# Residual sum and normalising steps at other places on VectorE, feed-forward products at the end of each pair's work on TensorE

## What is computed

```python
for i in range(DEPTH):        # DEPTH = 6, HEADS = 16, DIM_HEAD = 64, WINDOW = 32
    x = attn_layer(shift_tokens(x), Wqkv[i], q_scale[i], k_scale[i], Wo[i]) + x
    x = ffn_layer(shift_tokens(x), ln_g[i], ln_b[i], W1[i], b1[i], W2[i], b2[i]) + x

def ffn_layer(x, g, bln, W1, b1, W2, b2):
    mu = x.mean(-1, keepdims=True)
    var = ((x - mu) ** 2).mean(-1, keepdims=True)
    xn = (x - mu) / jnp.sqrt(var + 1e-05) * g + bln
    hg = xn @ W1 + b1                      # 128 -> 2 * 341
    a, gate = jnp.split(hg, 2, -1)
    return a * jax.nn.gelu(gate, approximate=False) @ W2 + b2
```

## Time and profile before

| | us |
|---|---|
| median of 3 runs | 6589.64 |
| lowest, highest | 6587.38, 6609.08 |
| the profiled execution | 6594.14 |
| its span | 6592.5 |
| PE busy in the span | 5401.5 |
| DVE busy in the span | 4045.7 |
| ACT busy in the span | 2755.0 |

### The profile page before, as it was taken

The page is one execution under the profiler, slowest core; times in us unless marked ns, Lnnn a source line. Parts: engine busy times, 40 slices in busy tenths (PEclk is TensorE's granted clock), DMA queues, the critical chain, the costliest instruction groups (busy, mean ns, idle before and its releaser), DMA issues. The chain is left out here.

```text
span 6592.5 us, 170288 instructions
## 1 busy us (share of the span) xinstructions
PE 5401.5 (82%) x71376; PEld 3458.5 (52%) x71376; DVE 4045.7 (61%) x6338; ACT 2755.0 (42%) x5035; POOL 2357.1 (36%) x2148
## 2 busy tenths in 40 slices
PE   6877778686868768888888888888888888888884
PEld 4756657484846554444444444444444444444442
DVE  6464656555564656666666666666666666666662
ACT  3132232313132315555555454455555555455552
POOL 2132222222222324444444444444444444444440
PEclk8787878796878879999999999999999999999997
DMA  0000000000000002222222222222222222222221
GB/s 17 4 1 4 1 4 1 4 1 4 3 2 4 1 34 60 57 55 67 62 56 56 60 64 56 53 64 62 57 57 64 64 56 56 59 63 55 55 50 37
DMA packets 255851, 252.33 MB, mean 38 GB/s; under 512 B 29680, under 2 KB 248688, under 8 KB 254704
## 3 DMA queue, kind: packets, MB, share of 16 engines
q1 hardware_dynamic: 255088, 241.29, 14.5%
HBM read 29.90 MB, written 4.19 MB: 5 GB/s over the span
## 5 line engine op out<-in xcount | busy, mean ns | idle before, releaser
L1245 POOL TENSOR_TENSOR turn<-prod 128x512 f32<-128x512 f32 x768 | 977.4, 1273 | 1872.0 <-PE banks L1018 998.7
L988 PE MATMUL banks<-w2s,xs 128*128 128x512 f32 x2304 | 1290.0, 643 | 62.6 <-DVE xs L1317 54.8
L1285 DVE TENSOR_TENSOR prod<-banks,tabs 128x1024 f32<-128x1024 f32 x768 | 936.6, 1219 | 138.7 <-ACT sq L1132 137.3
L1254 POOL TENSOR_TENSOR turn<-turn,rs 128x512 f32<-128x512 f32 x768 | 794.4, 1055 | 450.7 <-ACT rs L1149 449.2
L1132 ACT ACTIVATE sq<-banks 128x512 f32<-128x512 f32 x768 | 458.5, 597 | 967.4 <-PE banks L988 967.0
L583 POOL TENSOR_TENSOR ao<-at,msk 128x512 f32<-128x512 f32 x288 | 390.7, 1367 | 1013.7 <-PE banks L360 534.1
L1018 PEld LDWEIGHTS banks<-msk,turn 128*128 128x128 f32 x3072 | 349.2, 142 | 533.2 <-issue 518.2
L1296 DVE TENSOR_REDUCE ss<-sq 128x8 f32<-128x512 f32 x768 | 519.4, 676 | 1.5
L1066 PE MATMUL banks<-ot,w2s 128*128 128x512 f32 x768 | 413.3, 621 | 126.8 <-DVE y L1354 123.3
L988 PEld LDWEIGHTS banks<-w2s,xs 128*128 128x128 f32 x2304 | 382.4, 201 | 235.4 <-DVE xs L1317 61.9
L1018 PE MATMUL banks<-msk,turn 128*128 128x128 f32 x3072 | 478.6, 279 | 2.5 <-ACT ot L1177 1.6
(11 more groups left out here) (204 smaller groups left out, 9741.6 us busy)
## 6 DMA issues: line engine op xcount, KB each, us to landing
v<-v_tok SPq DMA_DIRECT2D x1152, 132.0 KB, 2.5
v<-v_tok SPq DMA_DIRECT2D x384, 66.0 KB, 2.1
v<-v SPq DMA_DIRECT2D x188, 132.0 KB, 2.5
w2s<-in_weights SPq DMA_DIRECT2D x10, 768.0 KB, 4.8
tabs<-in_rot SPq DMA_DIRECT2D x40, 128.0 KB, 2.6
w2s<-in_weights SPq DMA_DIRECT2D x1, 2713.5 KB, 11.1
w2s<-in_weights SPq DMA_DIRECT2D x10, 256.0 KB, 3.0
xin<-in_x SPq DMA_DIRECT2D x8, 256.0 KB, 3.5
```

The lines of the kernel that those rows point to most:

```text
L988: pe.matmul(a_bank(use), xs[:, t % 2, b * P:(b + 1) * P], w[:, at:at + 512], start=True, stop=True).then_inc(a_done, 1)
L1245: gp.tensor_tensor(turn[:, r % ROTS, :, :].rearrange(halves, s=2), prod[:, r % 2, 0, :, :].rearrange(halves, s=2), prod[:, r % 2, 1, :, :] ...
L1254: gp.tensor_tensor(turn[:, r % ROTS, :, :], turn[:, r % ROTS, :, :], along(rs[:, q % 2, b, :], DH), ALU.mult).then_inc(rot_done, 1)
L1285: v.tensor_tensor(prod[:, r % 2, :, :, :], a_bank(use).rearrange("p (h d) -> p h d", h=HU).unsqueeze(1) .to_broadcast([P, 2, HU, DH]), tab ...
```

## The change

Nothing is added or taken away on any engine but the place of instructions. On PE and in the numbering `a_use` the feed-forward products come after `values`, and with them ACT's part, after its second `take_heads`. On DVE the residual sum is taken out of step 1 and becomes step 0, in pair 0, between the second `sums` and `normalise`; the copies to `xf` stay in pair 1 behind the second `rotate`; the steps 2, 5 and 6 go behind `normalise`; the inverse deviation, scale and shift go from pair 3 to pair 4 (k = 4), between the first `sums` and the second `rotate`.

```diff
@@ a_use, PE's order of the bank's uses
+            if feed:
+                a_use["x", g, 2] = len(a_use)
             for name in ffn_products(g):
                 a_use["c", g // 8 - 1, name] = len(a_use)
-            if feed:
-                a_use["x", g, 2] = len(a_use)
@@ PE
-                        for name in ffn_products(g):
-                            ffn(g // 8 - 1, name)
                         if feed:
                             project(g, 2)
                         if order:
                             turn_heads(order[1])
                         if attend:
                             values(g)
+                        for name in ffn_products(g):
+                            ffn(g // 8 - 1, name)
@@ ACT
-                        if 8 <= g:
-                            ffn(g // 8 - 1, g % 8)
...
                         if order:
                             take_heads(order[1])
+                        if 8 <= g:
+                            ffn(g // 8 - 1, g % 8)
@@ DVE
+                    def carry(t):
+                        if t % NT:
+                            v.tensor_copy(y1[:, :, 0:1], y1[:, :, P:P + 1]).then_inc(carry_done, 1)
+                        else:
+                            v.memset(y1[:, :, 0:1], 0.0).then_inc(carry_done, 1)
+
                     def ffn(t, k):
                         at = t % NT * P + 1
-                        if k == 1:
+                        if k == 0:
+                            carry(t)
                             v.wait_ge(o_done, 8 * t + 8)
-                            if t % NT:
...
                             v.wait_ge(carry_done, t + 1)
                             v.tensor_tensor(y1[:, :, 1:1 + P], blocks(out_bank), y[:, :, at:at + P],
                                             ALU.add).then_inc(res_done, 1)
+                        elif k == 1:
                             v.wait_ge(res_done, t + 1)
...
-                        elif k == 3:
+                        elif k == 4:
                             v.wait_ge(rstd_ready, t + 1)
...
                             sums(g, 0)
+                        if 8 <= g and g % 8 == 4:
+                            ffn(g // 8 - 1, 4)
+                        if feed:
                             rotate(g, 1)
-                        if 8 <= g:
+                        if 8 <= g and g % 8 == 1:
                             ffn(g // 8 - 1, g % 8)
                         if feed:
                             sums(g, 1)
+                        if 8 <= g and g % 8 == 0:
+                            ffn(g // 8 - 1, 0)
                         if attend:
                             normalise(g)
+                        if 8 <= g and g % 8 in (2, 5, 6):
+                            ffn(g // 8 - 1, g % 8)
```

More of the change, by code:

```diff
@@ L1343, in scale_table @@
                         v.tensor_tensor(tile, tile, w[:, W_S:W_1], ALU.mult).then_inc(tab_ready, 1)
+                    def carry(t):
[3 more added lines that the diff above has]
+                            v.memset(y1[:, :, 0:1], 0.0).then_inc(carry_done, 1)
                     def ffn(t, k):
                         at = t % NT * P + 1
-                        if k == 1:
+                        if k == 0:
+                            carry(t)
                             v.wait_ge(o_done, 8 * t + 8)
-                            if t % NT:
-                                v.tensor_copy(y1[:, :, 0:1], y1[:, :, P:P + 1]).then_inc(carry_done, 1)
-                            else:
-                                v.memset(y1[:, :, 0:1], 0.0).then_inc(carry_done, 1)
                             v.wait_ge(carry_done, t + 1)
```

## The result

The changed kernel takes 6361.12 us (median of 4 runs, 6355.04 to 6365.21) beside 6592.37 for the kernel before: ratio 0.9644, 95% interval [0.9624, 0.9664]. That is outside the range of the prediction (6185 to 6345) and 130 us above its number. The profiled execution has a span of 6356.3 us.

A forecast was written before the change was run, and what follows sets the result against it. PE was taken to set the pace, other engines mattering only through its waits. Terms: 123 + 138 + 103 = 364 us saved, 11 given back, 6 gained, so 359 off 6589.6 gives 6231 us; range 6185 to 6345.

The forecast's parts named there:

- the two waits: PE's waits in `output` for the residual sum and before pair 4's scores (L997) go: gains of 123 and 138 us.
- the order of starts by which the residual sum should be hidden: Pair 0: the sum (0.69 us) fits DVE's 1.42 us idle before `normalise`, as the eighth `output` starts before `values`; cost nothing.
- what is moved and costs nothing, with its cover: Instructions moved in pairs 1, 2, 4, 5, 6 fit idle time, such as DVE's 1.42 us behind the second `sums`; cost 0.
- the rotation in pair 4: DVE's second rotation, behind the moved scale and shift (1.19 us), ends before the first gate product: cost 0, bound 24 us.
- 11 given back for `xs`: End of pair 1: PE's wait for `xs` shows in each tile, 35 us against 24, bounded by 0 and 25.
- the clock's return: Tiles' stage: 70 stretches at PE's lower clock, all put down to the two long waits, vanish: gain 103 us.
- The gate pair becomes the new hold-up: Rival, chance 0.10: in pair 4 late rotation and table load cost 85 us, 6316; with the clock 70 more, 6386.
- the table load: ACT's second table load, after the gate products, just in time before its next square: 0; wholly exposed, 61 us.
- the clock that it added behind the gate wait: Part of a rival (0.10): idle time in the gate pair also lowers PE's clock in each tile, 70 us more, 6386.
- The residual wait that moves: Rival, chance 0.04: the sum in pair 0 waits and holds `normalise`, as much as before with its clock: 190 us, 6421.
- the pauses in each pair: Rival, chance 0.03: PE drains instructions faster than they come; each of 384 pairs pauses 2.2 us in its bursts, 6984.
- a clock that stays down as before: Rival, chance 0.07: other idle time within the tile keeps PE's clock down, losing the 103 us gain: 6334.

The follow-up runs named there:

- short POOL: Changed kernel with POOL's two operations of the pair done for one head of eight, part of the computation left out: 6282.35 us, ratio 0.9526 to the kernel before.
- sum_back: Changed kernel with the residual sum put back in pair 1, in front of the copies to `xf`: 6481.55 us, ratio 0.9823 to the kernel before.

## Why the prediction was wrong

**Right: the two waits.** 123.3 and 138 us were to go; 123.3 and 135.2 went, and the order of starts by which the residual sum should be hidden held: in pair 0 it ends at 3889.22, before `values` does, for which DVE then still waits 0.54 us (changed kernel, all engines):

```profile
3888.53 0.69 DVE L1357 TENSOR_TENSOR y<-banks,y 128x512 f32<-128x512 f32 x1
...
3888.86 0.86 PE L1043 MATMUL banks<-v,pt 64*32 64x66 f32 x64
...
3889.66 0.39 PE L997 MATMUL banks<-kmask,idb 128*128 128x256 bf16 x2
3889.76 0.21 DVE L1331 RECIPROCAL rc<-banks 128x8 f32<-128x8 f32 x1 [0.54 <-PE banks L1043]
```

**Wrong: the step "what is moved and costs nothing, with its cover".** It took the durations as they stood in the trace before, whatever POOL did beside them: 1.19 us for the product with the inverse deviation and the scale and shift, which had no POOL work beside them there, and 1.37 for the two copies, of which the first was already 0.42 longer for it. At the new places they take 2.50 and 1.85 (3897.03 to 3898.88), more than the cover of 1.42 us. The prediction had 0 for the rotation in pair 4, bounded by 24 us, and its wait is 26.8; it had 11 given back for `xs`, bounded by 25, and 24.6 came, with the clock behind it besides. Taken away by the short POOL, all this is 79 us; measured against the miss of 128, three fifths, though a part of the 79 is the wait for `xs` that the prediction had allowed for.

**Wrong in part: the size of the clock's return.** 103 us were put for it, 70 stretches at the lower level. The trace has a record of the granted clock, and counted there the kernel before is at the lower level for 259 us of the 4000, in 71 stretches, and the changed kernel for 72 us of the 3765, in 21. That is 187 us less, at 1.46 us in 3.41 some 80 us. Putting the stretches before down to the two waits was right: 43 of the 71 begin in or close behind the wait of L997, 25 at that of `output`, 3 at a pause in `scores`. The step that failed is that nothing would take their place. In the changed kernel 12 of the 21 begin at a pause, as in this pair 1, which no wait disturbs, and 6 at the wait for `xs`:

```profile
3968.78 0.43 PE L1004 MATMUL banks<-kx,qt 64*32 64x64 f32 x26
3971.30 0.75 PE L1004 MATMUL banks<-kx,qt 64*32 64x64 f32 x38 [2.08 <-issue]
3971.98 2.07 PE L988 MATMUL banks<-w2s,xs 128*128 128x512 f32 x2
```

```profile
3971.61:3975.02 3.41, 3.41 (x34) 2.10 (x13) 1.68 (x3) 0.67 (x2) 0.00 (x0) 0.50 0.00 0
```

The projection takes 2.07 us there and 1.13 in the plain pair. Of this term's 23 us a part belongs to the 79 above, since with the short POOL only 24 us at the lower level are left.

**Left out: the products' own place.** Five groups in 48 tiles at 0.16 to 0.20 us are some 40 us that the prediction took as nothing. A second count agrees: PE's busy time in the stage fell by 38 us (3533.38 to 3495.49), where the clock alone would take 80 away, so PE is busy for some 42 us more with the same products. That this weighs in the total is argued: the run that took three groups back gained nothing by itself. And why the place has its price is open.

**The sum after the fact**: 123 + 135 + 80 gained, 25 (`xs`), 27 (rotation), 4 (pauses: 98.3 to 102.2) and 42 (place) lost, is 240; the spans differ by 236. As the place's term is what PE's busy time leaves over, the sum has to come near; its test is that the 42 agree with the 40 from single pairs.

**The rivals.** "The gate pair becomes the new hold-up", with 6316 to 6386, is the one whose number held the result. That was mostly luck. It named the rotation that is late for the bank, without the reason, and for that its 24 us are near the 26.8. The other 61 were for the table load, which cost nothing (in the changed kernel ACT's first square of pair 5 starts at 3933.17, 2.26 us behind L997 at 3930.91; in the plain pair it is 2.27), and the clock that it added behind the gate wait did not come: none of the 21 stretches lies behind it. The residual wait that moves, the pauses in each pair, and a clock that stays down as before did not come either.

## What to carry to other kernels

Before moving an instruction of DVE, look at what POOL does at the new place, and take its duration from a row with that neighbour; a spread between least and median of one line, or two equal instructions of unequal length, shows such a neighbour before anything is built. A slack of 1.4 us is no cover for two instructions that may double. And where an engine has an idle time each round (here POOL from its last operation of one pair to the first sum of the next, for 4.85 us in the rows of pair 1 and 3.70 in pair 4, and DVE for 1.8 us before the sum with the down product), that is the place for them: three moves of a few lines gave 92 us.

## What the runs showed of the hardware

A COPY or TENSOR_SCALAR of DVE that lies in SBUF, and a TENSOR_TENSOR with both inputs there, take 1.15 to 1.39 us when they start beside a POOL TENSOR_TENSOR and 0.42 to 0.69 alone. A TENSOR_TENSOR with one input in PSUM (1219 ns for L1285, 692 for L1357) and a TENSOR_REDUCE (676 ns, L1296) take as long beside POOL as alone. POOL is held up in its turn: two operations took 2.68 us and not 2.04. And PE's granted clock can fall behind a pause of 2.08 us, and need not: of 47 waits of some 2.7 us it fell at 33 (sum_back). In the kernel before and the changed one no stretch at the lower level follows the gate's wait of 1.28 us.
